# GpSimd's packing additions in a graph network kernel: waits for counts of expanded adjacency tiles ahead of each pair of additions

## What is computed

```python
for _ in range(5):
    s_in  = state @ in_W.T  + in_b
    s_out = state @ out_W.T + out_b
    a_in  = Af @ s_in
    a_out = Af.T @ s_out
    a = concatenate([a_in, a_out, state])
    r = sigmoid(a @ r_W.T + r_b)
    z = sigmoid(a @ z_W.T + z_b)
    h_hat = tanh(concatenate([a_in, a_out, r * state]) @ h_W.T + h_b)
    state = (1 - z) * state + z * h_hat
out = tanh(state @ o1_W.T + o1_b) @ o2_W.T + o2_b
return layernorm(x + out)
```

## Time and profile before

| what | value |
|---|---|
| median of three runs | 731.83 us (728.74, 731.83, 732.44) |
| span of the profiled execution | 729.6 us |
| PE busy | 694.2 us, 95% |
| DVE busy | 483.7 us, 66% |
| ACT busy | 238.9 us, 33% |
| POOL busy | 123.8 us, 17% |
| mean granted clock of PE | 0.982 |

### The profile page before, as it was taken

How to read it: one execution, slowest core, us unless ns; L and a number is a source line. 1 busy time by engine, 2 the same in 40 slices (tenths; PEclk the granted TensorE clock), 3 DMA queues, 4 the chain that set the end, 5 groups by cost and what they waited for, 6 DMA issues and landing times.

```text
span 729.6 us, 8541 instructions
## 1 busy us (share of the span) xinstructions
PE 694.2 (95%) x3168; PEld 575.3 (79%) x3168; DVE 483.7 (66%) x747; ACT 238.9 (33%) x369; POOL 123.8 (17%) x94
## 2 busy tenths in 40 slices
PE   7999999787999999999999999999999999998991
PEld 7878888566888888888888888888888888886881
DVE  4777767898866458754555865455586556657884
ACT  1755544422112215311222431222143112213553
POOL 0022013999940000000000000000000000005052
PEclk9999999979899999999999999999999999999997
DMA  8763632000000000000000000000000000030003
GB/s 283 259 225 107 201 104 69 1 0 1 0 1 1 0 1 1 0 0 0 0 0 0 0 0 0 0 0 0 0 0 1 0 1 1 0 115 1 1 1 117
DMA packets 18412, 27.25 MB, mean 37 GB/s; under 512 B 1872, under 2 KB 9424, under 8 KB 18384
## 3 DMA queue, kind: packets, MB, share of 16 engines
q1 hardware_dynamic: 16864, 26.48, 11.0%
q10 hardware_dynamic: 1520, 0.40, 0.3%
HBM read 24.78 MB, written 2.10 MB: 37 GB/s over the span
## 4 chain that ended last, share of the span: by engine, by line
PE 83%; DVE 10%; ACT 2%; DMA 2%; issue 1%; ACTq 0%; DVEq 0%; SPq 0%
PE bank L452 36%; PE bank L395 14%; PE bank L397 14%; PE bank L396 14%; PE bank L424 2%; PE bank L535 1%; DVE a L825 1%; DVE rows L806 1%; DMA a<-in_L_gnn_r_W_dram 1%; PE bank L547 1%; DVE work L867 1%; DVE work L873 1%; DMA stage<-in_adj_dram 1%; DVE ring L811 1%; DVE stateT L892 1%
## 5 line engine op out<-in xcount | busy, mean ns | idle before, releaser
L452 PE MATMUL bank<-ring,rows 128*128 128x512 f32 x1280 | 297.1, 392 | 1.1 <-ACT ring L620 0.9
L452 PEld LDWEIGHTS bank<-ring,rows 128*128 128x128 f32 x1280 | 240.6, 189 | 51.7 <-ACT ring L620 1.6
L654 ACT ACTIVATE work<-work,bias 128x512 f32<-128x512 f32 x120 | 86.6, 724 | 294.3 <-DVE work L867 293.6
L867 DVE SCALAR_TENSOR_TENSOR work<-degree,deg_w,bank 128x512 f32<-128x512 uint16 x120 | 88.8, 743 | 111.6 <-PE bank L397 111.1
L811 DVE CAST ring<-a 128x1024 fp32r<-128x1024 uint8 x128 | 97.8, 774 | 13.0 <-PE bank L452 13.0
L395 PE MATMUL bank<-u_c,fold 128*128 128x512 f32 x240 | 97.7, 407 | 3.3 <-DVE work L867 3.3
L397 PE MATMUL bank<-u_c,fold 128*128 128x512 f32 x240 | 94.6, 394 | 0.0
L396 PE MATMUL bank<-u_c,fold 128*128 128x512 f32 x240 | 94.6, 394 | 0.0
L357 POOL TENSOR_TENSOR a<-a,o_bb 128x1024 f32<-128x1024 f32 x4 | 10.9, 2760 | 448.4 <-DMA a<-in_x_dram 448.4
L395 PE MATMUL bank<-st_c,own 128*128 128x512 f32 x160 | 63.1, 394 | 3.1 <-DVE st_c L806 3.1
L397 PE MATMUL bank<-st_c,own 128*128 128x512 f32 x160 | 63.1, 394 | 0.0
(11 more groups left out here) (121 smaller groups left out, 803.0 us busy)
## 6 DMA issues: line engine op xcount, KB each, us to landing
stage<-in_adj_dram SPq DMA_DIRECT2D x28, 512.0 KB, 5.2
work<-in_x_dram SPq DMA_DIRECT2D x1, 2048.0 KB, 15.9
a<-in_x_dram SPq DMA_DIRECT2D x1, 2048.0 KB, 8.1
a<-in_adj_dram SPq DMA_DIRECT2D x3, 512.0 KB, 11.2
out_dram<-a SPq DMA_DIRECT2D x3, 512.0 KB, 3.0
a<-in_L_gnn_r_W_dram SPq DMA_DIRECT2D x1, 768.0 KB, 6.8
a<-in_L_gnn_z_W_dram SPq DMA_DIRECT2D x1, 768.0 KB, 8.9
stateT<-in_L_gnn_h_W_dram SPq DMA_DIRECT2D x1, 768.0 KB, 10.4
```

Of the source, the lines that this page charges most:

```text
L452: last = nc.tensor.matmul(u_bank[2 * (c % 2) + d][:, :], rows[:, part, j, d * P:(d + 1) * P], ring[:, p % RING, jj, :], start=(j == 0 and ...
L654: nc.scalar.activation(gates[:, g, e, :], gates[:, g, e, :], ACT.Tanh if g == H else ACT.Sigmoid, bias=bias[:, g, e:e + 1]).then_inc(gate_ ...
L867: nc.vector.scalar_tensor_tensor(out=gates[:, g, e, :], in0=degree[:, c * CW:(c + 1) * CW], scalar=deg_w[:, g, e:e + 1], in1=g_bank[s % 3] ...
```

## The change

Ahead of each pair of packing additions POOL now waits for a count of expanded pairs. `n // 2` numbers the 28 pairs of additions from 0 to 27, and `PACE` is (4 - 1) x 32 // (2 x 2 x 7) = 3. The counts are thus 35, 38, 41, ... up to 116. No other engine's program is changed.

```diff
         PACK = 8
         NPK = NB // PACK
+
+
+        PACE = (LAST - 1) * S_PAIR // (2 * NPK * (PACK - 1))
         flat_stage = stage[:, :, :, :].rearrange("p s a w -> p (s a w)")
...
                     for k in reversed(range(PACK - 1)):
                         twice = block_of(PACK - 1) if k == PACK - 2 else acc
+                        pool.wait_ge(pair_ready, S_PAIR + PACE * (n // 2 + 1))
                         wait(pool, packed, n)
                         add(acc, twice, twice, packed)
                         pool.wait_ge(packed, n + 1)
```

## The result

| kernel | median us | runs |
|---|---|---|
| before | 730.74 | 728.74 to 732.44, 4 runs |
| changed | 713.79 | 711.30 to 714.08, 4 runs |

The ratio is 0.9766, with a 95% interval of 0.9734 to 0.9798: 2.3% faster. The profiled execution of the changed kernel took 714.08 us with a span of 712.0, so 2.1 us lie around the span, as the prediction had carried over. The span itself is 1.7 us longer than the 710.3 foretold.

A forecast was written before the change was run, and what follows sets the result against it. The prediction took TensorE (PE) to bound the kernel, with 19.6 us lost to late DVE work at the end of step 0. Span 729.6 - 19.6 + 0.3 = 710.3, plus 2.2 carried over: 712.5 us, range 708.5 to 720.

The forecast's parts named there:

- The loss of the stretch, 19.6 us: From step 0's transposes to step 1's first gate product: two pieces lose 19.6 us against the same pieces one step later.
- the same three waits: PE's waits on DVE: low state of chunk 3 (3.1 us), update of chunk 2 (3.2), update of chunk 3 (4.2).
- The cause: POOL's additions without a gap slow DVE: expansions take 1391 ns instead of 686, low parts of the state 1663 instead of 683.
- What stays in step 0: End of step 0: none of the loss stays once the additions are spread; all 19.6 us taken as gained.
- What arrives in steps 1 to 3: Spread additions stall PE by 0.3 us, at count 68 on the low state parts; bounds 0 and 29.2 us.
- the slack of 1.7 us: Start of the gates of chunk 3: low state ready at 286.05 us, wanted by PE at 287.73.
- fall where DVE waits for PE: Steps 1 to 3: claim for all counts other than 68, 98, 53 and 101.
- spreading spares DVE nothing in total: DVE's total cost from the additions, 29.2 us for 28 pairs, was to stay the same when spread.
- The sum: Whole kernel: span 729.6 - 19.6 + 0.3 = 710.3 us, with 2.2 us carried over 712.5; chance 0.82.
- Rival 2: One or two tight places stall in earnest, 5.4 us each with the clock: 717.9 or 723.3 us; chance 0.11.
- Rival 3: Step 0's extras and the additions at count 35 keep the first piece slow; only 6.75 us return: 725 us; chance 0.03.
- rival 4: Additions' cost to DVE not hidden at the ring of four expanded pairs: 29.2 us appear, 741.4 us; chance 0.04.

The follow-up runs named there:

- the second experiment: Changed kernel with all 56 additions in a row from count 65, the burst's old place in the cycle one step later: 731.11 us.
- third: Changed kernel without the 56 additions, the symmetry test's count of differences multiplied by zero: 714.63 us.
- tenth: Kernel before the change with each of the 56 additions replaced by a memset of the same output, count of differences multiplied by zero: 712.74 us.
- The seventh experiment: Changed kernel with POOL's four residual additions in the last step spread by waits too, instead of back to back: 708.81 us.
- the first experiment: Changed kernel with all 56 additions in a row from count 41, in the middle of step 1: 726.97 us.
- the fourth experiment: Changed kernel with the four counts in the gates of chunk 2 (35, 65, 68, 98) put off to the fifth pair: 712.99 us.
- 5: Changed kernel with one pair of additions for every two expanded pairs instead of three: 715.15 us.
- the sixth: Changed kernel with each of the 56 additions waiting for a count of its own, in steps of 1.5 expanded pairs: 712.59 us.

## Why the prediction was right

**The loss of the stretch, 19.6 us.** Measured 19.55: this step holds in mechanism and size. The comparison with the same two pieces one step later carried it, and the second experiment showed what the comparison could only suggest: put there, the burst brings the same three waits to the pieces that had been clean.

**The cause.** That DVE's operations last longer because of POOL had been argued from the earlier trace rows against the earlier trace rows, and from the end of the slow means where the additions end. The second, third and tenth experiments show it: without additions the expansions have a mean of 688 ns over the whole kernel; with a later burst they take 687 ns ahead of it and 1411 under it; and memsets, which read nothing, leave the operations with two inputs in SBUF at 0.69 us. A memset is also shorter than an addition, so the tenth run makes it likely, and doesn't prove, that it is POOL's reading that counts for these. It is also the rule of the Trainium skill, page "SBUF — State Buffer", section "Who interferes with whom", that two SBUF inputs contend only with a GpSimd operation that reads while a fast copy contends with any; the tenth run agrees with it, up to 1.00 us for the expansions and 0.69 for the others. The expansion behaves as the fast copy here; it handles 1024 columns in the 0.69 us that the others take for 512.

**What stays in step 0: nothing.** So it was: the first pair of additions ran from 135.0 to 137.9 us, the low parts of the state behind it were on time, and the update of chunk 2 ended at 146.1 us where PE came at 147.3.

**What arrives in steps 1 to 3.** 0.3 us were foretold, at count 68 and at no other, on the low part of the state; 0.48 of idle time came at just that count and part, 0.8 us with its restart. The place and the slack of 1.7 us held, and no other place shows a wait. That the sizes agree so well is partly luck. The delay of 2.0 us was put down to the pair at 68 alone; it cost 1.36, and the pair at 65, which the prediction counted among those that "fall where DVE waits for PE", left the 0.80 that made the stall. One sentence there was off: that spreading spares DVE nothing in total. It spared 9 of 29 us. The expansions were met as much as before (97.8 and 98.5 us in all, means of 774 and 779 ns, near the 0.77 foretold), but the updates never: their three lines took 73.1 us in the kernel before and 63.0 in the changed one, 685 ns in the mean at L893 and at L896.

**The sum.** 712.5 foretold, 713.79 measured. The term that was missing lies outside the stretch: I read the waits of PE only from 126 to 210 us and carried the rest of the execution over unchanged. In it was a wait of 3.0 us of the same kind, and the clock behind it can fall or not; it cost the profiled execution 1.7 us that it had not cost before. The 0.5 us too little for the stall and this 1.7 are 2.2 us; the start-up, 0.6 us shorter by chance, hid a part, and the span came out 1.7 above the forecast. The seventh experiment, which took the wait away, gained 5.0 us in the median and 5.5 between the profiled executions, where the wait makes 3.2 and the clock 1.7.

**The rivals.** Rival 2 happened in small (one stall of 0.5 us, and no clock dip behind it). Rival 3 fell with the changed kernel's first piece, 31.18 us where it needed one near 44, and the second experiment excludes step 0's extras as a cause. For rival 4, the slower one, the point at which it decides was 0.70 us of loss per pair of additions; measured was 0.8 / 28 = 0.03.

## What to carry to other kernels

Where background work on one engine lengthens another engine's operations, ask of it not how long it takes but how many of its instructions meet the other engine in a chain with little slack, and what an earlier meeting has left over: the same 56 instructions cost 17 us in one burst over the end of a step, 13 us in one burst in the middle of a step (726.97 - 713.79), and 0.8 us in the profile, nothing that the medians can tell, in pairs paced by a counter that the other engine raises anyway. Price such a stretch by the same work one iteration later, then read the waits of the bounding engine over the whole execution and not only there: the same pattern stood a second time in the last step and was worth another 5 us.

## What the runs showed of the hardware

A wait of PE of about 3 us may or may not be followed by a lower clock. The wait on a gate in the last step, 2.9 to 3.1 us long, stands in nine of the profiled executions. In six of them (the changed kernel and experiments 1, 3, 4, 5 and 10) the clock of the ten microseconds behind it was 0.71 to 0.85, and the rest of the execution from that matmul on took 60.7 to 61.8 us; in three (the kernel before and experiments 2 and 6) it was 1.00, and the rest took 59.0 to 59.3. Length does not sort them: the wait of 2.9 us in the fourth experiment has a dip behind it, the one of 3.1 us in the sixth has none. What decides it stays open. In the changed kernel the dip was to 1.2 GHz and back to 2.4:

```profile
652.40:655.40 3.00, 3.00 (x9) 2.31 (x8) 1.82 (x3) 1.50 (x3) 0.00 (x0) 0.50 0.00 0
655.80:661.00 5.20, 5.20 (x25) 4.26 (x24) 5.07 (x9) 3.48 (x7) 0.00 (x0) 1.00 0.01 3
```

All eight waits of 3.1 to 4.5 us that the dense additions caused, three in the kernel before, two in the first experiment and three in the second, had matmuls at 1.2 GHz (0.50) behind them. Stalls of 0.5 to 0.9 us had none right behind them in any run.

GpSimd's memset of 128 x 512 words took 0.53 us and slowed only the expansions (0.69 to 1.0 us), and was itself held up to 1.0 us where the two met. Its addition on the same shape took 1.0 to 1.8 us. One of 128 x 1024 took 2.7 us, and under it single DVE operations lasted 2.1 and 2.9 us.
